# Two-layer graph attention: gathered rows in a ring of 24, and VectorE's masks ahead in layer 0's first steps

## Chip, cores and metric

One core of a Trainium2 chip. The metric is the device time of one launch in microseconds. The core's engines are TensorE (PE; PEld is its weight load), VectorE (DVE), ScalarE (ACT), GpSimd (POOL) and SyncE (SP, which only issues transfers). Each works through its own list of instructions in order, and semaphores order them against each other.

## What is computed

Two attention layers over a graph of 8192 nodes with 256 features. The adjacency (8192 x 8192, int32) is symmetric and sparse: about 8 neighbours a row, and the node itself.

```python
h = jnp.maximum(_layernorm(x), 0.0)
Wh = h @ W
e = (Wh @ a[:256])[:, None] + (Wh @ a[256:])[None, :]
att = softmax(where(adj == 0, -1e9, e), axis=1)
x = x + leaky_relu(att @ Wh, 0.2)                    # layer 0
h = jnp.maximum(_layernorm(x), 0.0)
e = leaky_relu(h @ a1[:256] + (h @ a1[256:]).T, 0.01)
att = softmax(where(adj > 0, e, -9e15), axis=1)
x = x + att @ h                                      # layer 1
```

## The kernel before

Nodes go in 64 tiles of 128 rows. All order on an engine is written out by hand, in the order in which the Python code emits the instructions.

**Layer 0** takes tile t per step. SyncE loads the tile's adjacency in four quarters of 1 MB; ScalarE converts them (`convert`) to eight-bit floats; VectorE folds eight adjacency columns into one byte in four parts (`fold`, parts 0 to 3); TensorE transposes the folded words (`turn`, four transposes), ScalarE copies them out (`copy_words`), and VectorE unpacks them into the masks `adjT` with eight operations (`unpack`). TensorE multiplies these masks with the 64 tiles of V in 128 matmuls (`aggregate`, L973); the turn of the next tile, t + 1, stands inside, behind matmul pair `turn_at`, and waits for the last fold part of tile t + 1 (L963). An aggregate of tile t waits for `adjT_ready` of t and for `ysb_ready` of t - 2, which is ScalarE's copy of the sums off the accumulator that t will reuse (L975 to L977; `copy_sums` L528).

VectorE's `step(t)` (L838) does, in order: `normalise(t-1)`, a reciprocal behind the sums of tile t - 1; fold part 0 of t + 2, behind its conversion; `extract(t+1)`, the neighbour lists out of the keys; `add_x(t-1)`, behind `copy_sums`; `unpack(t+1)`, behind `copy_words`; parts 1 and 2; `scale_h`, behind ScalarE's root; part 3; `decode`, one list of a group of four, and for every fourth tile also the bits of all four (steps 2, 6, 10 and so on); `make_keys(t+2)`; `dots(t-1)`, behind ScalarE's `finish`. ScalarE's step (L535) has the quarters of t + 3 with `copy_words(t+1)`, `copy_sums(t-1)`, the root and `finish` between them: quarter 0, words, sums, quarter 1, root, quarter 2, finish, quarter 3.

**Between the layers** the 44 tiles from tile 20 on are sorted by number of neighbours.

**Layer 1** does the first 20 tiles as dense attention on TensorE and the other 44 by gathering each node's neighbours. The dense part runs over 5 groups of 4 tiles, each in 16 chunks of 64 matmuls, 80 chunks in all. For each chunk ScalarE makes signs (L1300), in two halves, each waiting for TensorE to be done with the half four back; VectorE makes the negative and the positive mask (L1473, L1478); TensorE waits for the positive mask (L1620) and multiplies (L1639).

The gathered part has 420 rows of slots (a slot is one neighbour of each of 128 nodes): 24 in the first tile of nodes, down to 4 in the last. GpSimd issues one indirect DMA per slot (L1264), 128 x 258 numbers, into `gat`. They are grouped in 88 batches of at most 6 (`BS`); batch k lies in buffer k mod 4 (`NBUF`), and before its first gather GpSimd waits until the batch four back has been added (L1262). ScalarE takes the two exponentials of a batch (`weights`, L1313), VectorE their larger (`larger`, L1509) and then, per slot, adds the weighted row (`add_row`, L1518); `rows_by` says how many rows VectorE has added by each chunk, some 5 a chunk (7 in the first 16), put around the negative and the positive mask. `LEAD = 3` is by how many rows the weights go ahead. The sum of a finished tile is closed in the next tile's rows 2 to 4 (`join`, `divide`, `add_x1`, which raises `so_ready`). GpSimd scatters a finished tile to the output (`scatter`, L1253, waits for `so_ready`) after it has issued the batch that stands `OUT_LAG = 5` batches behind the tile's last (L1268).

## Time and profile before

| | before |
|---|---|
| median of 3 runs | 1916.56 us (1912.78 to 1921.1) |
| profiled execution | 1914.35 us, of it 1912.5 us span |
| TensorE busy | 1691.5 us (88%), granted clock 0.93 of full |
| VectorE busy | 1203.0 us (63%) |
| ScalarE busy | 973.4 us (51%) |
| GpSimd busy | 651.6 us (34%) |

Layer 0's projection and statistics fill the first 105 us, its 64 tiles stand from 105 to 1058, layer 1 from 1067 to the end. The page cuts the span in 40 slices of 48 us:

```profile
PE   6888999999999999999999397677888888978878
DVE  7488888988888888674444377652435445435434
ACT  5987665665666556666662375432333233323322
POOL 0000000000000000026665548755656657665562
PEclk9998999999999999999999698877889889979889
```

A digit is the busy share of the slice in tenths. PE is full in most of layer 0 and isn't in layer 1, where the clock row shows that it also ran below full clock. A busy share alone doesn't say what bounds a stage: that is read from which wait ends last.

### The profile page before, as it was taken

How to read it: one execution, taken by the hardware profiler on the slowest of the kernel's cores; microseconds unless marked ns; L12 is line 12 of the kernel's file. 1: busy time of each engine (PE TensorE's matmuls, PEld its weight loads, DVE VectorE, ACT ScalarE, POOL GpSimd, SP SyncE). 2: the span in 40 equal slices, each digit the busy share in tenths (PEclk: the TensorE clock that was granted, in tenths of full speed). 3: DMA queues.
4: the chain of work that ended last, by engine and by line, in shares of the span. 5: the costliest groups of instructions: out<-in, count | busy, mean ns of one | idle time of the engine just before them, and what ended most of it. 6: DMA issues, size and time to landing. Idle time of an engine off the chain costs nothing. (4 is left out here: it accounts for less than half of the span.)

```text
span 1912.5 us, 37724 instructions
## 1 busy us (share of the span) xinstructions
PE 1691.5 (88%) x13955; PEld 1391.3 (73%) x13955; DVE 1203.0 (63%) x4595; ACT 973.4 (51%) x1367; POOL 651.6 (34%) x607
## 2 busy tenths in 40 slices
PE   6888999999999999999999397677888888978878
PEld 5646888888888888888888285454666667757657
DVE  7488888988888888674444377652435445435434
ACT  5987665665666556666662375432333233323322
POOL 0000000000000000026665548755656657665562
PEclk9998999999999999999999698877889889979889
DMA  8529998888988889989994534533333333433331
GB/s 287 182 76 386 342 349 325 314 311 321 354 320 326 318 310 331 355 333 378 386 379 104 130 94 134 160 80 88 101 89 83 111 89 94 117 100 99 88 92 52
DMA packets 142801, 410.60 MB, mean 215 GB/s; under 512 B 26193, under 2 KB 90066, under 8 KB 109906
## 3 DMA queue, kind: packets, MB, share of 16 engines
q1 hardware_dynamic: 108434, 329.85, 47.6%
q0 software_dynamic: 27904, 73.43, 13.9%
q10 hardware_dynamic: 6336, 5.77, 1.0%
q8 instruction: 62, 1.02, 0.2%
q14 instruction: 65, 0.53, 0.1%
HBM read 368.94 MB, written 40.03 MB: 214 GB/s over the span
## 5 line engine op out<-in xcount | busy, mean ns | idle before, releaser
L984 PE MATMUL banks<-HV,adjT 128*128 128x257 f16 x8192 | 938.8, 274 | 16.7 <-DVE adjT L658 8.8
L984 PEld LDWEIGHTS banks<-HV,adjT 128*128 128x128 fp8e4 x8192 | 792.5, 98 | 148.2 <-DVE HV L688 23.7
L1639 PE MATMUL banks<-Vp,adjp 128*128 128x257 f16 x2560 | 540.6, 292 | 115.4 <-issue 59.2
L1639 PE MATMUL banks<-Vn,adjn 128*128 128x257 f16 x2560 | 538.1, 291 | 48.9 <-issue 47.7
L1264 POOL DMA_INDIRECT gat<-h_of_layer,rec x420 | 465.8, 1109 | 275.5 <-issue 117.9
L444 ACT ACTIVATE adj_f<-adj_i 128x2048 fp8e4<-128x2048 int32 x256 | 480.1, 1898 | 6.6 <-DMA adj_i<-in_adj 6.5
L1300 ACT ACTIVATE adjn<-h1bc,nh 128x512 fp8e5<-128x512 f32 x320 | 212.1, 716 | 446.2 <-remote 272.1
L1639 PEld LDWEIGHTS banks<-Vp,adjp 128*128 128x128 fp8e4 x2560 | 261.2, 103 | 192.3 <-issue 126.5
L1639 PEld LDWEIGHTS banks<-Vn,adjn 128*128 128x128 fp8e4 x2560 | 262.2, 103 | 124.8 <-issue 76.5
L425 POOL DMA_DIRECT2D HV<-x_after_layer x44 | 25.5, 580 | 773.4 <-DVE rank L911 741.3
L1473 DVE TENSOR_TENSOR adjn<-adjp,adjn 128x1024 uint16<-128x1024 uint16 x80 | 55.4, 692 | 334.8 <-ACT adjn L1300 296.0
L1534 DVE SCALAR_TENSOR_TENSOR sacc<-gat,w,sacc 128x257 f32<-128x257 f32 x332 | 152.5, 477 | 0.0
L492 ACT ACTIVATE pk<-banks 128x512 uint16<-128x512 uint16 x64 | 37.9, 593 | 170.3 <-PE banks L969 143.9
L695 DVE RECIPROCAL rden<-banks 128x1 f32<-128x1 f32 x64 | 10.7, 168 | 145.9 <-PE banks L984 115.3
L655 DVE TENSOR_SCALAR adjT<-pk 128x512 uint16<-128x512 uint16 x448 | 94.6, 282 | 0.0
L957 PE MATMUL banks<-w_sb,hT 128*128 128x257 f32 x256 | 68.9, 392 | 15.6 <-ACT hT L456 15.3
L627 DVE SCALAR_TENSOR_TENSOR fold<-adj_f 128x1024 int32<-128x1024 int32 x64 | 77.2, 1206 | 7.4 <-ACT adj_f L444 7.4
L418 POOL DMA_INDIRECT x_after_layer_sorted<-HV,rank x44 | 66.5, 1512 | 13.4 <-issue 12.2
L525 ACT ACTIVATE hh<-x,nmr,rstd 128x256 f32<-128x256 f32 x64 | 38.4, 601 | 53.6 <-DVE nmr L727 45.8
L1515 DVE TENSOR_TENSOR w<-e 128x5 f32<-128x5 f32 (+2 forms) x88 | 13.9, 157 | 77.8 <-ACT e L1321 58.5
L519 ACT ACTIVATE std<-mv,eps 128x1 f32<-128x1 f32 x64 | 18.8, 294 | 86.0 <-DVE mv L719 83.9
L1255 POOL DMA_INDIRECT out<-sout,rec x44 | 46.5, 1058 | 43.1 <-DVE sout L1550 31.8
(158 smaller groups left out, 1395.2 us busy)
## 6 DMA issues: line engine op xcount, KB each, us to landing
adj_i<-in_adj SPq DMA_DIRECT2D x256, 1024.0 KB
h_of_layer<-hh SPq DMA_DIRECT2D x64, 129.0 KB
hs<-h_of_layer SPq DMA_DIRECT2D x64, 129.0 KB
xt<-in_x SPq DMA_DIRECT2D x64, 128.0 KB
packed_adj<-pk SPq DMA_DIRECT2D x64, 128.0 KB
x_after_layer<-x SPq DMA_DIRECT2D x64, 128.0 KB
HV<-in_x SPq DMA_DIRECT2D x14, 512.0 KB, 8.8
gat<-h_of_layer,rec POOLq DMA_INDIRECT x420
```

Source lines behind the costliest of these rows:

```text
L418: pool.indirect_dma_start(x1s_d, bass.IndirectOffsetOnAxis(ap=rank[:, m:m + 1], axis=0), HV[:, T + m % SH, 0:D], None).then_inc(xs_out[m % ...
L444: nc.scalar.activation(adj_f[:, b, q * QC:(q + 1) * QC], adj_i[:, q, :], ACT.Copy, scale=2.0, saturate=False).then_inc(conv_done, 1)
L627: nc.vector.scalar_tensor_tensor(four, whole[:, 0:4 * GW], 1, whole[:, 4 * GW:8 * GW], ALU.logical_shift_right, ALU.bitwise_or)\
L655: last = nc.vector.tensor_scalar(adjT[:, b, i, :], pk[:, pb, :], PAIR << i, 6 - i, ALU.bitwise_and, ALU.logical_shift_left)
L957: last = nc.tensor.matmul(wps[t % 3][:, 0:DV], hT[:, t % 2, c, :], w_sb[:, c, :], start=(c == 0), stop=(c == 1))
L984: last = nc.tensor.matmul(acc[b][:, 0:DV], adjT_h[:, b, i, q, :, h], V0[:, jb, s, 0:DV], start=(jb == 0 and s == 0), stop=(jb == T - 1 and ...
L1255: pool.indirect_dma_start(out, bass.IndirectOffsetOnAxis(ap=rec[:, m, OWN:OWN + 1], axis=0), sout[:, m % NOUT, :], None).then_inc(so_out[m ...
L1264: pool.indirect_dma_start(gat[:, k % NBUF, s - s0, :], None, h_d, bass.IndirectOffsetOnAxis(ap=rec[:, m, s:s + 1], axis=0))\
L1300: i = nc.scalar.activation(adjn_b[:, c % 2, jb // 2, :, jb % 2], h1bc[:, g2, :], ACT.Relu, scale=-BIG, bias=nh2[:, tiles[j]:tiles[j] + 1], ...
L1473: nc.vector.tensor_tensor(part, both, part, ALU.bitwise_and).then_inc(neg_ready, 1)
L1534: nc.vector.scalar_tensor_tensor(acc, x, w, acc, ALU.mult, ALU.add)\
L1639: mm = nc.tensor.matmul(bank[2 * i + part][:, 0:DV], m[:, i * P:(i + 1) * P], V[:, j, s, 0:DV], start=(j == 0 and s == 0), stop=(j == T - ...
```

## The change

Two parts, one in each layer.

In layer 0, VectorE's steps 1 to 6 (`HURRY = 7`) put `unpack(t+1)`, `extract(t+1)` and fold part 0 of t + 2, in that order, behind `normalise`, ahead of `add_x`. And TensorE's turns inside tiles 2 and 3 stand behind matmul pair 48 and 32 of 64, not behind pair 4; tile 1's stays at 48, and from tile 4 on it is pair 4 again.

In layer 1, `gat` becomes a ring of 24 rows. The gather of row q waits until row q - 24 has been added, one wait per row. A batch that would cross the ring's end is cut there, which makes 101 batches of the 88. `NBUF = 6` batches have a landing semaphore each, and a batch also waits until the one six back has been added. `lead_of` lets the weights of a batch go ahead only when the batch before it has begun. Three semaphores of `take_sums` become one.

```diff
--- before.py
+++ after.py
@@ -82,6 +82,7 @@
     XB = 4
     LAG = 5
     XL = 1
+    HURRY = 7
     UN = 4
     VU = 16
     NPK = 4
@@ -836,15 +837,19 @@
                         decode_end(e)
 
                 def step(t, j, n_in, x1_reuse, kept, off, ahead=True, folds=True, listed=False,
-                         taken=False, e=None):
+                         taken=False, e=None, hurry=False):
 
                     normalise(t - 1, (j - 1) % 2)
-                    if folds:
+                    if hurry:
+                        unpack(t + 1, (j + 1) % 2, (j + 1) % NPK)
+                        extract(t + 1, (j + 1) % UN)
                         fold(t + 2, j % 2, 0)
-                    if taken:
+                    elif folds:
+                        fold(t + 2, j % 2, 0)
+                    if taken and not hurry:
                         extract(t + 1, (j + 1) % UN)
                     add_x(t - 1, (j - 1) % NX, n_in, x1_reuse, kept, off)
-                    if ahead:
+                    if ahead and not hurry:
                         unpack(t + 1, (j + 1) % 2, (j + 1) % NPK)
                     if folds:
                         fold(t + 2, j % 2, 1)
@@ -922,7 +927,7 @@
                 dve.wait_ge(hh_ones, 1)
                 for t in range(1, T):
                     step(t, t % UN, *counts(t), ahead=t + 1 < T, folds=t + 2 < T, listed=t + 2 < NS,
-                         taken=t + 1 < NS, e=(t - 2) // UN if 2 <= t < NS + 2 else None)
+                         taken=t + 1 < NS, e=(t - 2) // UN if 2 <= t < NS + 2 else None, hurry=t < HURRY)
                     if t == SORT:
                         sort_totals()
                     if t == SORT + 1:
@@ -1001,7 +1006,9 @@
                 pe.wait_ge(ones_set, 2)
                 aggregate(0, 0, v0_wait=True, reuse=False, turn_at=None)
                 aggregate(1, 1, reuse=False, turn_at=3 * T // 4)
-                with pe.Fori(1, SORT // 2) as k:
+                aggregate(2, 0, turn_at=3 * T // 4)
+                aggregate(3, 1, turn_at=T // 2)
+                with pe.Fori(2, SORT // 2) as k:
                     for b in range(2):
                         aggregate(k * 2 + b, b)
                 for b in range(2):
@@ -1032,7 +1039,8 @@
         RB = 4
         BIG = 2.0 ** 100
         BS = 6
-        NBUF = 4
+        RING = 24
+        NBUF = 6
         LEAD = 3
         FIRST = 1.35
         HEAD = 3.0
@@ -1044,7 +1052,10 @@
         for m in range(NS):
             parts = -(-slots[m] // BS)
             for i in range(parts):
-                batch.append((m, slots[m] * i // parts, slots[m] * (i + 1) // parts))
+                s0, s1 = slots[m] * i // parts, slots[m] * (i + 1) // parts
+                q = sum(slots[:m])
+                wrap = -(-(q + s0 + 1) // RING) * RING - q
+                batch.extend([(m, s0, s1)] if wrap >= s1 else [(m, s0, wrap), (m, wrap, s1)])
         row = [(m, s, k) for k, (m, s0, s1) in enumerate(batch) for s in range(s0, s1)]
         begin = [row.index((m, s0, k)) for k, (m, s0, s1) in enumerate(batch)]
         at = [sum(slots[:m]) for m in range(NS + 1)]
@@ -1056,7 +1067,8 @@
 
         def lead_of(q):
 
-            return sum(1 for b in begin if b < q + LEAD) if q < len(row) else len(batch)
+            return sum(1 for k, b in enumerate(begin)
+                       if b < q + LEAD and (k == 0 or begin[k - 1] < q)) if q < len(row) else len(batch)
 
         def ended(q):
 
@@ -1097,7 +1109,7 @@
             sS = early[:, 9 * T:9 * T + 2 * NS].rearrange("p (s t) -> p s t", s=2)
             tS = early[:, 11 * T:11 * T + NS]
             exc = early[:, 12 * T:12 * T + NS]
-            gat = sb("gat", [P, NBUF, BS, ROW], f32)
+            gat = sb("gat", [P, RING, ROW], f32)
             sacc = sb("sacc", [P, 2, 2, DV], f32)
             sout = sb("sout", [P, NOUT, D], f32)
             e8 = sb("e8", [P, 2, 2, BS], f32)
...
@@ -1258,11 +1268,13 @@
 
                 done = 0
                 for k, (m, s0, s1) in enumerate(batch):
-                    if k >= NBUF:
-                        pool.wait_ge(row_added, begin[k - NBUF + 1])
                     for s in range(s0, s1):
+                        q = at[m] + s
+                        free = max(q - RING + 1, begin[k - NBUF + 1] if k >= NBUF and s == s0 else 0)
+                        if free > 0:
+                            pool.wait_ge(row_added, free)
                         pool.indirect_dma_start(
-                            gat[:, k % NBUF, s - s0, :], None, h_d,
+                            gat[:, q % RING, :], None, h_d,
                             bass.IndirectOffsetOnAxis(ap=rec[:, m, s:s + 1], axis=0))\
                             .then_inc(gat_in[k % NBUF], 16)
                     while done < NS and last[done] + OUT_LAG <= k:
@@ -1318,7 +1330,7 @@
                     if k >= 2:
                         act.wait_ge(w8_ready, k - 1)
                     for i, scale in ((0, 1.0), (1, SLOPE1)):
-                        nc.scalar.activation(e8[:, k % 2, i, 0:s1 - s0], gat[:, k % NBUF, 0:s1 - s0, DV],
+                        nc.scalar.activation(e8[:, k % 2, i, 0:s1 - s0], gat[:, begin[k] % RING:begin[k] % RING + s1 - s0, DV],
                                              ACT.Exp, scale=scale, bias=hb[:, i, m:m + 1]).then_inc(e8_ready, 1)
 
                 def load_rows(m):
...
@@ -1523,7 +1535,7 @@
                     acc = sacc[:, m % 2, s % 2, :]
                     if i == 0:
                         dve.wait_ge(w8_ready, k + 1)
-                    x = gat[:, k % NBUF, i, 0:DV]
+                    x = gat[:, q % RING, 0:DV]
                     w = w8[:, k % 2, i:i + 1]
                     if s < 2:
                         if m >= 2 and s == 0:
```

## Rows read from the trace of the kernel before

**Rows 1.** windows of stages: length, busy us (instructions) per engine, clock, DMA share, GB/s

```profile
155.80:172.40 16.60, 16.59 (x131) 13.81 (x132) 14.46 (x59) 13.38 (x12) 0.00 (x0) 0.86 1.02 415
...
200.00:1058.00 858.00, 858.00 (x7798) 749.63 (x7797) 645.65 (x2860) 513.59 (x460) 137.74 (x132) 1.00 0.88 323
1330.00:1870.00 540.00, 458.54 (x3517) 355.53 (x3516) 238.76 (x701) 173.86 (x356) 336.46 (x316) 0.88 0.35 97
```

**Rows 2.** timeline, TensorE: start us, length us, what, count, idle before and releaser

```profile
145.97 1.05 PE L984 MATMUL banks<-HV,adjT 128*128 128x257 f16 x8
155.81 1.45 PE L984 MATMUL banks<-HV,adjT 128*128 128x257 f16 x6 [8.78 <-DVE adjT L658]
...
188.18 0.38 PE L969 MATMUL banks<-idb,fold 128*128 128x128 bf16 x4
```

**Rows 3.** timeline, VectorE, layer 0's steps 1 to 3

```profile
148.77 1.22 DVE L627 SCALAR_TENSOR_TENSOR fold<-adj_f 128x1024 int32<-128x1024 int32 x1 [6.67 <-ACT adj_f L444]
149.92 0.42 DVE L749 MAX8 ktop<-HV 128x8 f32<-128x256 f32 x1
...
152.42 0.42 DVE L706 SCALAR_TENSOR_TENSOR lr<-ysb 128x256 f32<-128x256 f32 x1
...
153.89 1.47 DVE L655 TENSOR_SCALAR adjT<-pk 128x512 uint16<-128x512 uint16 x7
...
159.18 0.17 DVE L695 RECIPROCAL rden<-banks 128x1 f32<-128x1 f32 x1
...
168.54 0.16 DVE L781 TENSOR_REDUCE fl<-ktop 128x1 f32<-128x8 f32 x1
...
177.54 0.67 DVE L647 TENSOR_TENSOR HV<-fold,keypos 128x512 f32<-128x512 uint16 x1
...
179.06 0.17 DVE L695 RECIPROCAL rden<-banks 128x1 f32<-128x1 f32 x1
```

**Rows 4.** timeline, ScalarE, the same steps

```profile
143.71 0.60 ACT L492 ACTIVATE pk<-banks 128x512 uint16<-128x512 uint16 x1 [0.29 <-PE banks L969]
...
151.35 0.46 ACT L532 ACTIVATE ysb<-banks,rden 128x256 f32<-128x256 f32 x1
...
162.04 0.58 ACT L492 ACTIVATE pk<-banks 128x512 uint16<-128x512 uint16 x1
```

**Rows 5.** timeline, VectorE, the first row added in layer 1

```profile
1110.61 0.35 DVE L1531 TENSOR_SCALAR sacc<-gat,w 128x257 f32<-128x257 f32 x1
```

**Rows 6.** timeline, GpSimd, two stretches of layer 1

```profile
1121.54 1.15 POOL L1264 DMA_INDIRECT gat<-h_of_layer,rec  x1 [22.88 <-DVE sacc L1534]
...
1124.39 3.28 POOL L1264 DMA_INDIRECT gat<-h_of_layer,rec  x1 [0.30 <-issue]
...
1403.01 0.94 POOL L1264 DMA_INDIRECT gat<-h_of_layer,rec  x1 [6.42 <-DVE sacc L1534]
...
1411.36 0.97 POOL L1264 DMA_INDIRECT gat<-h_of_layer,rec  x1 [0.30 <-issue]
```

**Rows 7.** who waited for whom, 1050 to 1913: us in total, times, longest

```profile
PEld banks L1639 <- issue: 203.0, 212, 15.6
...
POOL gat L1264 <- DVE sacc L1534: 115.8, 25, 22.9
...
POOL out L1255 <- DVE sout L1550: 31.8, 7, 10.8
```

**Rows 8.** windows between two stops of GpSimd, columns as above

```profile
1406.00:1409.00 3.00, 3.00 (x30) 2.62 (x28) 3.00 (x9) 0.22 (x2) 2.39 (x3) 1.00 0.50 150
...
1415.00:1418.00 3.00, 1.40 (x10) 0.79 (x9) 0.00 (x0) 0.00 (x0) 2.26 (x3) 1.00 0.32 89
```

**Rows 9.** the page's costliest groups: busy, mean ns of one, idle before

```profile
L1264 POOL DMA_INDIRECT gat<-h_of_layer,rec x420 | 465.8, 1109 | 275.5 <-issue 117.9
...
L1515 DVE TENSOR_TENSOR w<-e 128x5 f32<-128x5 f32 (+2 forms) x88 | 13.9, 157 | 77.8 <-ACT e L1321 58.5
```

**Rows 10.** instructions that touch the tile gat: ns min/median/max

```profile
L1321 ACT ACTIVATE e<-gat,hb x176: 282/287/310, 1082.7 to 1884.1; 128x5 f32<-128x5 f32 x66, 128x4 f32<-128x4 f32 x60, 128x6 f32<-128x6 f32 x40, 128x3 f32<-128x3 f32 x10
```

More of the change, by code:

```diff
@@ L1153, in two_layer_graph_attention @@
             evn_ready = sem("evn_ready")
-            den2_ready = sem("den2_ready")
-            den_ready = sem("den_ready")
-            rd_ready = sem("rd_ready")
+            den_steps = sem("den_steps")
             fac_ready = sem("fac_ready")
@@ L1483, in take_sums @@
                                             banks[:, :, D].rearrange("p (g s) -> p s g", s=2), ALU.mult)\
-                        .then_inc(den2_ready, 1)
-                    dve.wait_ge(den2_ready, g + 1)
+                        .then_inc(den_steps, 1)
+                    dve.wait_ge(den_steps, g * 3 + 1)
                     nc.vector.tensor_tensor(den[:, :], den2[:, 0, :], den2[:, 1, :], ALU.add)\
-                        .then_inc(den_ready, 1)
-                    dve.wait_ge(den_ready, g + 1)
-                    nc.vector.reciprocal(rd[:, :], den[:, :]).then_inc(rd_ready, 1)
-                    dve.wait_ge(rd_ready, g + 1)
+                        .then_inc(den_steps, 1)
+                    dve.wait_ge(den_steps, g * 3 + 2)
+                    nc.vector.reciprocal(rd[:, :], den[:, :]).then_inc(den_steps, 1)
+                    dve.wait_ge(den_steps, g * 3 + 3)
                     for s in range(2):
```

## Prediction, made blind

> **What bounds the kernel now.** I read the windows by stage first. From 200 to 1058 us TensorE never stops: 7798 matmuls in 858 us, 0.110 us each, at full clock [rows 1]. That is nearly all of layer 0, so a change there pays only through its start, before 200 us, and whatever TensorE loses there is never won back. The one hole is in front of tile 2: TensorE ends tile 1 at 147.0 and starts tile 2 at 155.8, released by the last of the eight mask operations [rows 2]. The tile then takes 16.6 us at a mean clock of 0.86 [rows 1] instead of the usual 132 x 0.110 = 14.5 (128 matmuls and the turn's four), so the hole cost 8.8 + 2.1 = 10.9 us. That is all the layer 0 part can win.
>
> Layer 1 is different. From 1330 to 1870 TensorE makes 3517 matmuls, 55 of the 80 chunks of 64, in 540 us: 9.8 us a chunk where 64 x 0.110 = 7.0 would do [rows 1]. The list of waits says what is missing: weight loads stood 203.0 us on "issue", with nothing to wait for, and GpSimd stood 115.8 us in 25 stops for rows to be added [rows 7]. The two belong together. In 1406 to 1409, shortly after a stop, GpSimd gathers and TensorE makes 10 matmuls a us; in 1415 to 1418, with GpSimd gathering at its quickest and VectorE idle, it makes 3.3 [rows 8]. By the timelines, each long slow stretch ends 1 to 3 us after GpSimd stops at its buffer limit. So there is a cycle: GpSimd runs, TensorE starves, no rows are added, the buffer fills, GpSimd stops, TensorE recovers. A gather is on GpSimd for 1.11 us in the mean [rows 9] and 0.30 us lie between two [rows 6]; 420 gathers and 44 scatters ask some 464 x 1.41 = 654 us of layer 1's 845 (1067 to 1912). GpSimd is nearly a second bound.
>
> **Layer 0, step 1.** Today VectorE's order is fold part 0 (which waits for converted adjacency until 148.8), extraction 149.9 to 152.4, add_x to 153.9, masks to 155.5 [rows 3]. The mask words lie ready at 144.3 [rows 4]. With masks first, they are done by 144.3 + 1.6 = 145.9, before tile 1 ends. What is late next: tile 2 also waits for the copy of tile 0's sums off its accumulator, and that ScalarE instruction runs 151.35 to 151.8, behind conversions that the change doesn't move [rows 4]. Tile 2 starts at 151.8, not 155.8: 4.0 us won, not 8.8. With a hole of 4.8 us I leave the cold-clock loss at 2.0 (bounds 0 and 2.1).
>
> **Steps 2 and 3, by the durations of [rows 3].** The turn of tile 3 now sits at 3/4 of tile 2, so at 151.8 + 10.9 + 2.0 = 164.7, its word copy (0.6 us) at 165.3; today the copy is done at 162.6 [rows 4]. VectorE finishes step 1 at 159.2 as today (its dots wait for ScalarE), and in the new order the next thing in its queue is masks 3, waiting for that copy. Queued behind them are extraction, fold 4, add_x and the decoding, and VectorE idles 6 us that it uses today. Then: masks to 166.9, extraction 2.5, fold part 0 1.15, add_x 1.7, parts 1 and 2 0.9, scale and part 3 0.8, making 173.9; decoding, 168.5 to 177.5 today, 9.0, and keys and dots 1.5: step 2 ends at 184.4, today 179.1. Tile 3 runs 168.0 to 182.6; masks 4 come at 184.4 + 1.7 = 186.1 (today they are 1 us ahead of tile 4). TensorE waits 3.5 us. Tile 4's turn comes 1.1 us into the tile, 187.2, and needs the finished fold 5. Its part 3 comes after extraction, part 0, add_x, parts 1 and 2 and scale: 186.1 + 7.0 = 193.1. Today it is ready half a us ahead of the turn at 188.2 [rows 2]. TensorE waits 5.9 us more. Tile 5 starts at about 206.2 with the clock's ramp, today 201.6: 4.6 us late. The next decoding of bits, in step 6, is still in the new order and costs tile 8 about 2 us again by the same sum. Layer 0 ends 6 to 8 us later than today. I take +7. If the turn of tile 5 did not wait, it would be about -1; if ScalarE's queue moved forward too, -8.
>
> **Layer 1, first release.** GpSimd stops after 24 gathers, at 1098.7, and goes on at 1121.5, when a batch of six is added [rows 6]. The first row is added at 1110.6 + 0.35 = 1111.0 [rows 5]; by the new rule gather 24 needs that row alone. Then each row frees one gather. VectorE waits for rows in 1138 to 1226, where GpSimd never stops, so the head start is kept: -10 us (bounds 0 and -10.5).
>
> **Layer 1, the ring in steady work.** The limits follow from the lists of rows in the code. Before, a batch's first gather needs the batch four earlier added: GpSimd is held 16.1 rows ahead on average for rows 200 to 299, 13.0 for 300 to 379. The ring alone would give 21.5 and 17.7. But the scatter of a finished tile stands five batches after its last batch on GpSimd's queue, and batches are cut at the ring's end: 101, not 88. Five batches are then fewer rows. The scatter of tile 22, say, stands after 290 gathers instead of 294, and needs the same row 277 added (it waits for the finished tile, five rows into the next). Behind it every gather waits. With this limit the means are 19.2 and 15.3, and at 40 of the 44 scatters the scatter is the tighter limit (21 before). So GpSimd is still stopped once a tile, which is about two chunks: as often as today, where 26 stops of over 1 us fall on these 55 chunks. No row is late there today, so that being further ahead feeds nobody. Value taken: 0. Bounds: each of some 25 stops could end on the first add of a chunk instead of the fifth, 4 x 0.4 = 1.6 us earlier, -40; or each of some 20 slow stretches could last one gather more, 1.25 us, of which TensorE loses 1.1: +22.
>
> **Small parts.** 13 more batches: two exponentials of 0.29 us [rows 10] and a maximum of 0.16 [rows 9] each, 9.6 us in all on ScalarE and VectorE, which both wait for TensorE in most chunks; taken +3, bounds 0 and 10. 300 more waits on GpSimd: the gather at 1411.4, a batch's first, has a satisfied wait before it and follows after the same 0.30 us as the others [rows 6], so nothing. One semaphore for three: same waits, nothing.
>
> Sum: 1914.35 + 7 - 10 + 0 + 3 = 1914.4 for the profiled execution. The median of the runs stands 2.2 above it, and I allow one more us for the second start of the clock after tile 4: 1917.5.
>
> **The Trainium skill.** A gather takes 0.94 us when VectorE idles and up to 3.28 when it is busy [rows 6]. The Trainium skill, "DMA: Bandwidth & Descriptors", section on SWDGE vs HWDGE vs iDMA, says that GpSimd writes the descriptors into SBUF state from which VectorE locks it out in its two-port mode; by that rule the trace agrees. On the slow stretches it speaks against my reading: "Runtime: NRT & Kernel Launch", section Instruction fetch mechanics, calls the crossing of a block of instructions mostly hidden. By that rule gathers would not starve TensorE, the depth of the ring would be worth nothing either way, and the sum would be the same as mine; the 203.0 us on "issue" [rows 7] say that something isn't hidden.
>
> **Rivals.** (B) Finer stops end the starving. A stop of 1 to 2 us is enough today to give TensorE 10 us of full pace; if the ring keeps GpSimd at its limit, every chunk has a short stop and the long slow stretches go. For it: the pace right after stops. Against it: the scatters. Half of the bound, -20: 1894 to 1898. (C) Slower, by one mechanism: in 1330 to 1870 the deeper ring lets GpSimd run on when TensorE is already starved, one gather more in each of 20 stretches, +22: 1917.5 + 22 = 1939; it decides from about half a gather more, when with layer 0's +7 the kernel is past +0.5%. For it: stretches end only with the stop, and were longest, about 25 us around 1240 and 1300, where GpSimd had most room. Against it: the scatter stops it once a tile. (D) Layer 0 does what the diff says: tile 2 at 151.8 and no later hole, -5 with a warm clock: 1905. Against it: the 6 us that VectorE idles. That the change doesn't do what it says is half of my forecast: the ring of 24 is held at 9 to 19 by the scatters.
>
> **Chances.** Forecast 0.46 (1908 to 1927), B 0.24, C 0.23, D 0.07. What a measurement here can tell from no change is about 0.5%, 9.6 us. Faster by more: B's 0.21, D's 0.05, 0.03 of the forecast: 0.29. Slower by more: C's 0.20 and 0.06 of the forecast: 0.26. Within: 0.45. The range leaves out the ends of B and C: 1893 to 1937.
>
> **What would show it.** Tile 2 starting at 151.8 after the copy of sums; a wait of 3 to 4 us before tile 4 and of 5 to 6 at its turn; layer 0 ending 6 to 8 us later. Gather 24 at about 1111 from layer 1's same start. In steady work, waits of GpSimd's scatter for the finished tile, 31.8 us in 7 today [rows 7], up to over 60 in more than 15, and "issue" of the weight loads within 20 us of 203. The prediction is wrong if "issue" falls by half (B) or rises by 20 (C), or if layer 0 shows no new hole.

## The result, and the profile after

The change makes the kernel slower: 1965.64 us, median of 5 runs (1952.13 to 1967.12), against 1917.0 for the kernel before beside it (5 runs), a ratio of 1.0225 with a 95% interval of 1.0178 to 1.0271. The whole interval is above 1, so it is slower; whether by less or more than 2% is open. The forecast was 1917.5 with a range that ended at 1937. The profiled execution took 1959.8 us, 45.5 more than before's 1914.35.

The page after, its line of TensorE, of GpSimd and of the granted clock in 40 slices of 49 us:

```profile
PE   6887999999999999999997588678788688877678
POOL 0000000000000000046672587855556455455552
...
PEclk9998999999999999999999789879899798878779
```

Layer 0 looks as before. In layer 1 TensorE shows more 6s and 7s, and in the last nine slices the clock shows three 7s where the kernel before has one. The windows of the same trace split it. Columns: stretch in us, its length, busy time and instructions of each engine, clock, DMA share, GB/s. Layer 1 is cut some 3 us before chunk 40 of 80 begins, at 1507 here and at 1518 in the kernel before:

```profile
1074.00:1507.00 433.00, 331.70 (x2527) 256.38 (x2528) 229.77 (x651) 183.41 (x402) 278.81 (x245) 0.86 0.42 113
1507.00:1949.00 442.00, 342.04 (x2593) 260.86 (x2591) 175.46 (x521) 126.51 (x268) 231.51 (x220) 0.84 0.29 82
1330.00:1870.00 540.00, 424.65 (x3278) 328.01 (x3277) 223.41 (x657) 165.46 (x351) 300.90 (x284) 0.87 0.32 88
```

The kernel before, cut at the same chunk (its row for 1330 to 1870 is in [rows 1]):

```profile
1067.00:1518.00 451.00, 341.85 (x2535) 260.16 (x2536) 228.42 (x645) 181.16 (x392) 285.15 (x252) 0.83 0.41 111
1518.00:1909.00 391.00, 331.10 (x2587) 260.06 (x2584) 177.82 (x527) 124.30 (x257) 227.43 (x213) 0.89 0.33 90
```

The first half got quicker, 451 to 433 us for the same 2530 matmuls. The second went from some 385 us (1518 to the last matmul at 1903.6) to 442 for the same 2590. Layer 1 as a whole, from its first gather to its last matmul, takes 874.7 us instead of 836.1, and it starts 7.0 us later (1074.5 instead of 1067.5). That is 45.6 us, all of the loss: 7 from layer 0, 18 won in the first half of layer 1, 57 lost in the second. The sum is firm. The split between the halves isn't: e1 below has the layer 1 of the kernel before and splits it otherwise.

The waits say who stands in it (engine, line, releaser: us in total, times, longest). The lines answer to [rows 7]:

```profile
PEld banks L1651 <- issue: 231.4, 254, 10.0
POOL out L1265 <- DVE sout L1562: 195.0, 30, 13.7
POOL gat L1276 <- DVE sacc L1543: 25.5, 8, 11.7
POOL gat L1276 <- DVE sacc L1546: 22.3, 47, 6.3
```

GpSimd's waits before a scatter rose from 31.8 us in 7 to 195.0 in 30, and its waits at a gather fell from 115.8 in 25 and 41.8 in 10 to 22.3 and 25.5. So the scatter is the limit now, once a finished tile. The weight loads' "issue" rose from 203.0 to 231.4.

**What a long run of GpSimd does to TensorE.** GpSimd's timeline around one scatter interval (start, length, operation, and in brackets the idle time before it and what ended it):

```profile
1714.24 1.19 POOL L1265 DMA_INDIRECT out<-sout,rec  x1 [4.34 <-DVE sout L1562]
...
1749.81 0.95 POOL L1276 DMA_INDIRECT gat<-h_of_layer,rec  x1 [0.30 <-issue]
1764.31 1.86 POOL L1265 DMA_INDIRECT out<-sout,rec  x1 [13.56 <-DVE sout L1562]
```

From 1714 to 1751 it never stops, and then it waits 13.6 us for a finished tile. The same stretch by windows of 4 us:

```profile
1722.00:1726.00 4.00, 4.00 (x39) 3.49 (x37) 1.35 (x4) 2.29 (x6) 2.93 (x4) 1.00 0.48 132
1726.00:1730.00 4.00, 4.00 (x37) 3.33 (x35) 1.77 (x5) 1.14 (x4) 3.09 (x4) 1.00 0.39 102
1730.00:1734.00 4.00, 1.65 (x9) 0.88 (x9) 3.00 (x11) 1.34 (x2) 3.39 (x3) 0.89 0.39 108
1734.00:1738.00 4.00, 3.36 (x15) 1.86 (x13) 0.00 (x0) 0.00 (x0) 3.09 (x4) 0.50 0.49 148
1738.00:1742.00 4.00, 2.73 (x12) 1.36 (x11) 0.00 (x0) 0.00 (x0) 3.01 (x4) 0.50 0.40 108
1742.00:1746.00 4.00, 1.36 (x6) 0.57 (x5) 0.73 (x3) 1.72 (x4) 2.86 (x4) 0.50 0.46 128
1746.00:1750.00 4.00, 0.58 (x2) 0.10 (x1) 2.10 (x6) 0.00 (x0) 3.09 (x4) 0.50 0.39 103
1750.00:1754.00 4.00, 1.15 (x5) 0.49 (x5) 0.00 (x0) 0.07 (x1) 0.76 (x1) 0.50 0.30 66
1754.00:1758.00 4.00, 4.00 (x25) 2.97 (x23) 0.00 (x0) 1.26 (x2) 0.00 (x0) 0.63 0.00 0
1758.00:1762.00 4.00, 4.00 (x39) 3.49 (x37) 1.64 (x5) 2.48 (x8) 0.00 (x0) 1.00 0.00 0
```

TensorE makes 39 matmuls in 4 us, then 9, 15, 12, 6, 2 and 5, and comes back to 39 only when GpSimd's column is 0. Nothing holds it that the profile can name. VectorE and ScalarE have little to do, the DMA engines are less than half busy, and the clock has dropped to its lower level (0.50) after TensorE began to idle, which makes the way back longer (25 in its first 4 us). This is the cycle of the prediction's first part, but with 27 gathers and scatters in one run.

How the long ones weigh: I counted the starts of the matmuls in steps of 2 us and summed the stretches in which TensorE made fewer than 5 a us, each at its length less 0.110 us a matmul. In the second half they cost the kernel before 86 us, of them 16 in the one stretch that lasted 15 us or more. In the changed kernel they cost 137, of them 109 in six such stretches, up to 28 us long. Of the 57 us that the second half lost, 51 are in such stretches.

The length of a run isn't all that counts. From 1183 to 1291 GpSimd goes 108 us without a stop of over 0.6 us, and TensorE falls and comes back several times in it, with GpSimd at work all the while:

```profile
1236.00:1240.00 4.00, 4.00 (x39) 3.49 (x37) 0.80 (x2) 2.81 (x8) 3.39 (x3) 1.00 0.94 274
1240.00:1244.00 4.00, 0.56 (x6) 0.25 (x3) 0.73 (x3) 0.49 (x2) 3.04 (x4) 1.00 0.77 251
```

In 1252 to 1256 it is at 37 again. It often comes back behind long gathers beside a busy VectorE (two of 2.6 us in the mean in 1232 to 1236). From 1268 on, with VectorE idle from 1272, it stays under 10 matmuls in 4 us until GpSimd stops. What lets it come back is open.

### The profile page after: what moved, and what is told of

Same layout as the page of the kernel before. It is cut to its first block and busy times, and to the rows that moved or that the text cites. A ratio compares the mean times of both kernels' runs of the same rounds, so it can differ in the third digit from the quotient of the medians.

```text
span 1957.8 us, 37793 instructions
## 1 busy us (share of the span) xinstructions
PE 1696.0 (87%) x13955; PEld 1389.5 (71%) x13955; DVE 1207.3 (62%) x4608; ACT 978.4 (50%) x1393; POOL 641.8 (33%) x607
## 5 line engine op out<-in xcount | busy, mean ns | idle before, releaser
L1276 POOL DMA_INDIRECT gat<-h_of_layer,rec x420 | 457.8, 1090 | 159.2 <-issue 111.4
L1265 POOL DMA_INDIRECT out<-sout,rec x44 | 52.2, 1186 | 200.3 <-DVE sout L1562 195.0
L1527 DVE TENSOR_TENSOR w<-e 128x5 f32<-128x5 f32 (+5 forms) x101 | 16.0, 159 | 95.8 <-ACT e L1333 75.9
L1333 ACT ACTIVATE e<-gat,hb 128x5 f32<-128x5 f32 (+5 forms) x202 | 46.5, 287 | 38.4 <-DMA gat<-h_of_layer,rec 38.4
```

Source lines behind the costliest of these rows:

```text
L1265: pool.indirect_dma_start(out, bass.IndirectOffsetOnAxis(ap=rec[:, m, OWN:OWN + 1], axis=0), sout[:, m % NOUT, :], None).then_inc(so_out[m ...
L1276: pool.indirect_dma_start(gat[:, q % RING, :], None, h_d, bass.IndirectOffsetOnAxis(ap=rec[:, m, s:s + 1], axis=0))\
L1333: nc.scalar.activation(e8[:, k % 2, i, 0:s1 - s0], gat[:, begin[k] % RING:begin[k] % RING + s1 - s0, DV], ACT.Exp, scale=scale, bias=hb[:, ...
```

## The experiments

Two kinds of chip turned up, told apart by what the kernel before takes. On one (the runs above, e1 to e4, e17 and e18) it takes 1916 to 1926 us. On the other (e5 to e16, three chips) it takes 1752. Every ratio is against the kernel before on the same chip.

For each kernel I also give the time that TensorE lost in the steady part of layer 1, from 1130 us to its last matmuls: the window's length less 0.110 us a matmul, the full pace of [rows 1]. For the kernel before and the changed one that is 773 - 4827 x 0.110 = 242 and 819 - 4885 x 0.110 = 282 us:

```profile
1130.00:1903.00 773.00, 634.25 (x4827) 489.60 (x4825) 368.32 (x1059) 267.90 (x565) 480.61 (x436) 0.87 0.36 100
```

```profile
1130.00:1949.00 819.00, 641.27 (x4885) 492.09 (x4883) 376.87 (x1088) 278.98 (x603) 479.43 (x435) 0.86 0.34 94
```

**One part alone: e1_layer0 and e2_ring.** e1 is the kernel before with layer 0's part of the diff. e2 is the changed kernel with that part undone:

```diff
-                         taken=t + 1 < NS, e=..., hurry=t < HURRY)
+                         taken=t + 1 < NS, e=..., hurry=False)
-                aggregate(2, 0, turn_at=3 * T // 4)
-                aggregate(3, 1, turn_at=T // 2)
-                with pe.Fori(2, SORT // 2) as k:
+                with pe.Fori(1, SORT // 2) as k:
```

> The kernel before with the layer 0 part alone. My step by step sum, which the trace after bears out (tile 2 starts early, then waits before tile 4 and in it), says layer 0 ends 6 to 8 us later and layer 1 is as before: 1922 to 1926 us where before has 1917. Rival: the start of layer 1 changes the course of its starving and recovering, and the time moves by more than 15 us.

> The kernel after with layer 0 put back as it was: the ring alone. If the parts add up, 1965.6 - 7 = 1955 to 1962 us. In the profile, GpSimd's scatter waits for the finished tile some 30 times and 190 us in all, and between such waits TensorE has slow stretches of over 15 us.

e1: 1929.68 us against 1915.67, ratio 1.0071 (1.0032 to 1.0110). e2: 1940.54 us, ratio 1.0119 (1.0049 to 1.0190). Both parts cost time, and their sum, 1.9%, agrees with the whole change's 2.25% within the intervals. e1's profiled execution is 12.6 us over before's (1926.93 and 1914.35): layer 1 starts 9.0 us later (1076.5 for 1067.5) and takes 3.6 us more (839.7 for 836.1, TensorE lost 248 us instead of 242). The median is 14 us over, where 5 to 9 were asked; the interval, 6 to 21 us, holds the 9 of layer 0's own stage, so a further price in layer 1 isn't shown. The ring's part is cheaper than expected (1955 to 1962 was asked of e2), but it has the changed kernel's marks:

```profile
PEld banks L1649 <- issue: 222.0, 249, 15.6
POOL out L1263 <- DVE sout L1560: 163.1, 24, 16.2
```

TensorE lost 264 us in it, between 242 and 282.

e1 also says how far one trace of layer 1 can be trusted. Its layer 1 is that of the kernel before, and yet chunk 40 begins 436 us after the first gather and the rest takes 404; in the kernel before it is 454 and 382, in the changed kernel 436 and 439. So the 18 us that the changed kernel won in its first half come without the ring too, and the halves move by some 20 us between executions of the same code. Layer 1 as a whole is steadier: 836.1 and 839.7 us without the ring, 874.7 and 857.8 (e2) with it. The same count of slow stretches over the whole steady part, for the runs on this kind of chip (each is a range, by where the steps of 2 us begin), beside the unbroken runs of GpSimd that lasted over 30 us, from 1330 us on (a stop of up to 1 us doesn't break a run):

| | slow stretches, us | of them in stretches of 15 us and over | GpSimd runs over 30 us |
|---|---|---|---|
| before | 201 to 208 | 57 to 87 | 1 |
| e1_layer0 | 209 to 213 | 49 to 70 | 1 |
| after | 237 to 248 | 131 to 145 | 4 |
| e2_ring | 223 to 226 | 91 to 119 | 5 |
| e3_scatter | 186 to 197 | 55 to 83 | 1 |
| e4_ahead14 | 181 to 188 | 27 to 63 | 2 |

e3 and e4 are the next two runs.

**The place of the scatters, and the depth: e3_scatter and e4_ahead14.** e3 is e2 with each scatter directly behind a wait that the ring makes anyway, so that no scatter brings a wait of its own in the steady part. e4 is e3 with GpSimd held 14 rows ahead instead of 24:

```diff
+        AHEAD = 24          # e4: 14
-                        free = max(q - RING + 1, begin[...] if ... else 0)
+                        free = max(free, q - AHEAD + 1, begin[...] if ... else 0)
                         if free > 0:
                             pool.wait_ge(row_added, free)
+                        while done < NS - 1 and free >= at[done + 1] + min(4, slots[done + 1] - 1) + 1:
+                            scatter(done)
+                            done += 1
...
-                    while done < NS and last[done] + OUT_LAG <= k:
-                        scatter(done)
-                        done += 1
```

> e2_ring with one edit: a scatter stands right behind the ring's own wait for the same row, so that it never holds GpSimd back further than the ring does. Ring, cuts and 101 batches stay. Theory S (the scatters turn the limit of 23 rows into a saw-tooth from 9 to 23, and GpSimd's long unstopped runs up the tooth starve TensorE): the long stretches go, 1885 to 1920 us. Theory D (being further ahead is itself the harm): GpSimd is now always about 23 ahead, so as slow as e2_ring or slower, 1955 to 1980. Theory B (the 13 extra batches cost it): as e2_ring, 1955 to 1962.

> e3_scatter with one number changed: GpSimd may be 14 rows ahead instead of 24, by the same wait per row. Theory S: what counts is that it stops often, not how far ahead: the same as e3_scatter within 15 us, 1885 to 1920. Theory D: faster than e3_scatter by 40 us or more, since it is less far ahead than ever before. If 14 rows are too few, VectorE's waits for weights go from 60 us to over 120 us and the time is over 1930.

e3: 1910.35 us, ratio 0.9968 (0.9935 to 1.0000). e4: 1891.13 us, ratio 0.9856 (0.9804 to 0.9907), faster than both kernels. Moving the scatters alone gives back 30 us of e2's time. The same 24 rows are there and the same 101 batches, so neither the ring's size nor the cut batches are the cause. The scatter theory asked for 1885 to 1920, the two others for 1955 and more. The waits of e3 and, below it, of e4:

```profile
PEld banks L1650 <- issue: 182.8, 229, 8.4
POOL gat L1278 <- DVE sacc L1545: 78.0, 45, 7.7
POOL out L1264 <- DVE sacc L1545: 44.3, 15, 8.2
```

```profile
PEld banks L1650 <- issue: 189.3, 238, 15.8
POOL gat L1278 <- DVE sacc L1545: 71.6, 57, 7.6
POOL gat L1278 <- DVE sacc L1542: 61.7, 19, 12.7
```

Now the gathers wait in many short stops (e4: 76 at a gather, 133 us), TensorE lost 229 us in each, and issue fell below before's 203. A limit of 14 is worth another 19 us by the medians, more than the scatter theory asked (15 at most) and half of what depth as the cause would have given (40). The steady part of the two traces doesn't show it, since e3's profiled execution was the quickest of its ten (1897.23).

Where the limit of 14 does show is the start of layer 1. Nothing has been added there, and GpSimd issues 24 gathers in a row (before) or 14 (e4). The same 4 us of the kernel before and of e4, whose first gathers went at 1067.5 and 1069.9:

```profile
1092.00:1096.00 4.00, 0.75 (x2) 0.21 (x2) 0.00 (x0) 0.00 (x0) 3.08 (x4) 0.53 0.75 117
1092.00:1096.00 4.00, 4.00 (x39) 3.49 (x37) 2.46 (x9) 2.91 (x7) 0.00 (x0) 1.00 0.40 112
```

Chunk 2 begins 44.7 us after the first gather in the kernel before (39 to 44 in e1, e2, e3 and the changed kernel, which all issue 24) and 30.7 us in e4. Of the 26 us by which e4's layer 1 is shorter than before's (810.2 and 836.1), 14 stand there, and 11 of them are left at chunk 10.

**Where TensorE doesn't starve: e5_uncut14, e8_masks1, e9_after, e10_ahead14, e16_ahead10.** e5 is the kernel before, 88 batches and four buffers, with e4's limit of 14 and its place of the scatters. e8 puts the masks first in step 1 alone (`HURRY = 2`, all turns as before). e9 is the changed kernel again and e10 is e4 again. e16 is e4 with `AHEAD = 10`.

> The kernel before with two edits in layer 1's GpSimd list: a wait per row that lets GpSimd be 14 rows ahead at most (its batch wait stays), and scatters behind that wait. Four buffers and 88 uncut batches as before. If the extra cuts cost nothing, the same as e4_ahead14, 1885 to 1898; if 13 batches cost their 9.6 us, 1875 to 1885; if it is the ring itself that helps e4_ahead14, 1905 or more.

> The kernel before with the masks first in step 1 alone, and TensorE's turns where they were. Step 1 by itself wins 4 us at tile 2; the turn of tile 3, one us into tile 2, then waits for the fold until about 157, and VectorE, which is late by then, sets tile 5 as before. Layer 0 ends within 2 us of before: 1913 to 1919. If the whole loss of e1_layer0 came from step 1, it would be 1925 or more.

> The changed kernel once more, beside the same kernel before as the next three. One chip gives the kernel before 1916 us and the other on which runs were made gives it 1752, with next to no stretches in which TensorE starves while GpSimd gathers (issue of the weight loads 43.6 us in e5). If this chip starves TensorE (before near 1916): ratio 1.022 to 1.029, issue 225 to 240 us, GpSimd's waits for the finished tile over 150 us. If it doesn't (before near 1752): theory S, by which layer 1's loss is TensorE starved in the long runs that the scatters allow, expects that only layer 0's part is left, 1.002 to 1.010, issue under 50; theory T, by which the scatters delay the rows themselves and the chip's kind doesn't matter, expects 1.020 to 1.030 here too.

> e4 once more, the ring held at 14 rows ahead and each scatter behind the ring's own wait for the same row, layer 0 as before. If this chip starves TensorE: 0.980 to 0.991 of the kernel before, issue 180 to 195. If it doesn't: theory S (all that the limit does is to take long starved stretches away) expects 0.998 to 1.006, since there is nothing to take away and the first release saves what 13 batches more cost; theory T expects 0.980 to 0.991 here too.

> e4 with the limit at 10 rows ahead instead of 14. 24 gave 1910 us and 14 gave 1891. If this chip starves TensorE and every row of room less takes from the starved stretches, 1870 to 1885 (ratio 0.977 to 0.984) and issue under 185; if rows come late before that helps, 1890 to 1930 with VectorE's waits for the exponentials over 150 us. If it doesn't starve: slower than before by 1 to 3%, since there the rows are what is late.

| | us | before beside it | ratio | 95% interval |
|---|---|---|---|---|
| e5_uncut14 | 1761.74 | 1751.88 | 1.0056 | 1.0036 to 1.0076 |
| e8_masks1 | 1755.42 | 1751.88 | 1.0011 | 0.9995 to 1.0027 |
| e9_after | 1755.44 | 1752.25 | 1.0014 | 0.9991 to 1.0037 |
| e10_ahead14 | 1762.01 | 1752.25 | 1.0051 | 1.0029 to 1.0073 |
| e16_ahead10 | 1839.78 | 1752.52 | 1.0492 | 1.0467 to 1.0516 |

The changed kernel costs 0.14% there, which the interval doesn't tell from nothing, and not 2.25%. That is a little under what the starving theory asked (1.002 to 1.010) and far from the other's 1.020. e4's gain of 1.4% is a loss of 0.5%, as that theory allowed. So the loss and the gain are both of TensorE starving. Here is the changed kernel on that kind of chip, 40 us in which GpSimd gathers without a stop, and its waits:

```profile
1400.00:1420.00 20.00, 20.00 (x183) 17.46 (x181) 10.75 (x32) 9.07 (x18) 15.43 (x16) 1.00 0.56 168
1420.00:1440.00 20.00, 20.00 (x183) 17.46 (x181) 12.82 (x37) 8.36 (x19) 15.73 (x15) 1.00 0.37 104
```

```profile
DVE w L1527 <- ACT e L1333: 173.5, 69, 7.2
PEld banks L1651 <- issue: 41.5, 19, 8.0
POOL out L1265 <- DVE sout L1562: 7.6, 5, 4.5
```

183 matmuls in 20 us are the full pace, beside 15 or 16 gathers. TensorE lost 89 us in the steady part (610 - 4734 x 0.110), GpSimd waits 7.6 us for finished tiles, and VectorE waits for rows instead. I take GpSimd to be the bound there, so that a limit of 14 or 10 only delays it: e10 lost 100 us and e16 172 (4.9% slower, where 1 to 3% was expected). The start of layer 1 fits too: 24 gathers in a row cost nothing here, chunk 2 begins 31.6 us after the first in e9 and 30.3 in e10. There is no run of e16 on the other kind of chip, so whether 10 would beat 14 there is open. e8's trace agrees with its tie: tile 2 starts at 154.3, and its turn then stands 2.57 us for the last fold. So masks first pay nothing that can be measured in step 1 alone either.

e15_uncut14 is e5 once more, on the same kind of chip again:

> The kernel before with its 88 batches and four buffers, a wait per row that holds GpSimd at most 14 rows ahead, and each scatter behind that wait. If this chip starves TensorE: if e4's gain comes from the limit and the place of the scatters, 0.980 to 0.992 of before; if it comes from the ring with its cut batches and its first release, 0.995 to 1.005. If it doesn't: 1.003 to 1.008, as e5.

1763.45 us, ratio 1.0065 (1.0043 to 1.0087), as e5. Whether the limit brings its gain without the ring is therefore open.

**Are the gathers the cause, and which side of them? e17_no_gathers and e18_narrow.** Both are e4 with the gathers changed. e17 issues only the first 24, and e18 fetches 43 numbers instead of 258 behind the first 24, from other rows of h than the layer's. In both the first 24 all fetch the first neighbour. The main lines:

```diff
e17:
-                        pool.indirect_dma_start(
+                        if q < RING:
+                            pool.indirect_dma_start(
e18:
+                        part = slice(0, ROW) if q < RING else slice(0, 43)
-                            gat[:, q % RING, :], None, h_d,
+                            gat[:, q % RING, part], None, h_d if q < RING else h_d.rearrange("r (k c) -> (r k) c", c=43),
```

> e13 again: e4 without the gathers behind the first 24, so the output isn't the layer's. If this chip starves TensorE (before near 1916): theory G (the gathers starve it) expects issue under 20 us and 1690 to 1760 us; theory P (a reason of TensorE's own) expects issue over 120 us and a time over 1830. If it doesn't (before near 1752): 0.967 to 0.973 of before.

> e14 again: e4 with 43 instead of 258 numbers in each gathered row behind the first 24, so the output isn't the layer's. If this chip starves TensorE: theory D (the gathers' number starves it) expects issue within 25 us of 189 and a time within 20 us of 1891; theory W (their bytes starve it) expects issue under 80 us and a time under 1811. If it doesn't: 1.000 to 1.006 of before.

Both ran on a chip that starves (before 1925.6 us). e17: 1696.95 us, ratio 0.882 (0.8719 to 0.8921). Its issue is 26.8 us, a little over the 20 asked for, and TensorE lost 39 us. e18: 1906.66 us, ratio 0.9902 (0.9859 to 0.9945), with issue at 170.4. The same 310 us of both and of e4, in the order e17, e18, e4:

```profile
1330.00:1640.00 310.00, 303.74 (x2735) 264.12 (x2733) 188.86 (x565) 140.46 (x298) 27.56 (x25) 1.00 0.12 38
```

```profile
1330.00:1640.00 310.00, 255.70 (x1996) 199.38 (x1995) 139.10 (x404) 99.61 (x206) 187.94 (x178) 0.90 0.16 38
```

```profile
1330.00:1640.00 310.00, 263.39 (x2042) 202.27 (x2042) 140.01 (x407) 102.12 (x210) 193.82 (x181) 0.90 0.35 97
```

Without gathers TensorE makes 2735 matmuls and its clock stays at 1.00. With narrow ones it makes 1996, hardly other than 2042 with whole rows, although the DMA engines' share has gone from 0.35 to 0.16 and the traffic from 97 to 38 GB/s. In the steady part it lost 248 us (e4 229). So the gathers starve TensorE, and by their being issued, not by their bytes. Whether it is their number, GpSimd's work on each or something that goes with both, these runs don't separate.

The same two edits had run before on the other kind of chip, without gathers as e6, e11 and e13, narrow as e7, e12 and e14:

> e4_ahead14 without the gathers after the first 24 rows (and these 24 all fetch the first neighbour), so its output is not the layer's: VectorE and ScalarE weigh and add what lies in the ring. If GpSimd's gathers are what starves TensorE, the weight loads' idle time on issue falls from 190 us to under 40, chunks take 7.1 to 7.6 us, and the time is 1660 to 1710 us. If the cause lies in TensorE's own instruction stream or in VectorE's and ScalarE's order, the slow stretches stay and the time is over 1780.

> e4_ahead14 with gathers of 43 numbers a row instead of 258 after the first 24 (from h seen as rows of 43, so wrong rows, and the output is not the layer's): one sixth of the bytes, as many instructions and descriptors. Theory issue (the descriptors that GpSimd writes are what starves TensorE): as e4_ahead14, 1880 to 1900, with issue still at 150 to 200 us. Theory bytes (the moved data are): 1700 to 1780, with issue under 80.

> e10 without the gathers behind the first 24, so the rows added are old ones and the output isn't the layer's. If this chip starves TensorE: theory G (the gathers starve it) expects issue under 20 us and 1690 to 1760 us, 130 to 200 less than e10; theory P (TensorE is slow in these stretches for a reason of its own: its clock, its own fetching, the dense part's waits) expects issue still over 120 and at most 60 us less. If it doesn't: 0.965 to 0.975, as e6.

> e10 with 43 instead of 258 numbers in each gathered row behind the first 24, so the output isn't the layer's: as many gathers and descriptors with a sixth of the bytes. If this chip starves TensorE: theory D (the number of descriptors, or GpSimd's writing of them, starves it) expects issue within 25 us of e10's and the time within 20 us; theory W (the bytes, which fill the DMA engines, starve it) expects issue under 80 us and at least 80 us less than e10. If it doesn't: within 0.5% of e10, as e7's profiled execution was within 0.5% of e5.

> e4 without the gathers behind the first 24, so the output isn't the layer's. If this chip starves TensorE (before near 1916): theory G (the gathers starve it) expects issue under 20 us and 1690 to 1760 us; theory P (a reason of TensorE's own) expects issue over 120 us and a time over 1830. If it doesn't (before near 1752): 0.967 to 0.973 of before, as e6 and e11.

> e4 with 43 instead of 258 numbers in each gathered row behind the first 24, so the output isn't the layer's: as many gathers and descriptors with a sixth of the bytes. If this chip starves TensorE: theory D (their number starves it) expects issue within 25 us of 189 and a time within 20 us of 1891; theory W (their bytes starve it) expects issue under 80 us and a time under 1811. If it doesn't: 0.998 to 1.006 of before, as e7 and e12.

Without gathers: 1699.74, 1699.51 and 1701.07 us, ratios 0.9695, 0.9697 and 0.9698. Narrow: e12 1759.58 (1.0031, 1.0005 to 1.0057) and e14 1759.34 (1.0033, 1.0018 to 1.0049), with issue at 40.9 and 48.5 us as in e10 with whole rows (41.5). Of e7's two executions one took 1756.96 us and the other 6685.42, which nothing here explains, and its median isn't used. Without gathers the two kinds of chip are alike, 1697 and 1700 us. So the 165 us between them arise only beside the gathers.

## Why the prediction was wrong, step by step

**Layer 0: the term was right, +7, its split wasn't.** TensorE's timeline of the changed kernel, where tile 0 starts 0.7 us earlier than before. It answers to [rows 2]:

```profile
150.49 13.81 PE L989 MATMUL banks<-HV,adjT 128*128 128x257 f16 x98 [4.19 <-issue]
186.24 1.76 PE L989 MATMUL banks<-HV,adjT 128*128 128x257 f16 x10 [3.83 <-DVE adjT L659]
193.01 0.59 PE L974 MATMUL banks<-idb,fold 128*128 128x128 bf16 x4 [5.02 <-DVE fold L642]
193.40 16.26 PE L989 MATMUL banks<-HV,adjT 128*128 128x257 f16 x128
```

Tile 2 at 150.5 (predicted 151.8), 3.83 us in front of tile 4 (3.5), the turn of tile 5 at 193.0 after 5.0 us (193.1 after 5.9): the queue behind the masks worked as worked out. Tile 5 came at 208.4, not 206.2, since the 128 matmuls behind the turn took 16.3 us instead of 14.1, a second start of the clock. The prediction left it out of the 206.2, which is 193.1 and 118 full-pace matmuls, and put it at one us in the last sum. The further 2 us at tile 8 never came: its masks end at 251.6 and it starts at 252.0. So two errors of 2 us cancel, and that the term came out at 7 is in part luck. From tile 0 on, tile 20 is 7.7 us later than before. Rival D is out. Layer 1 starts 7.0 us later in the changed kernel and 9.0 in e1.

**First release: right as an event, its worth not shown.** It answers to [rows 6]:

```profile
1117.34 0.94 POOL L1276 DMA_INDIRECT gat<-h_of_layer,rec  x1 [11.70 <-DVE sacc L1543]
1121.31 0.94 POOL L1276 DMA_INDIRECT gat<-h_of_layer,rec  x1 [3.02 <-DVE sacc L1543]
```

Gather 24 goes 42.9 us after gather 0, before 54.1 us: 11.2 earlier, 10 predicted. Whether TensorE won them isn't shown. Chunk 16 begins 185.4 us after the first gather in the changed kernel and 203.6 in the kernel before, but 189.0 in e1, which has no ring. On the kind of chip that doesn't starve, the changed kernel's layer 1 (e9) is 5.5 us shorter than that of the kernel before (in e8): 670.5 and 676.0.

**Small parts: right as far as they can be seen.** ScalarE is busy 978.4 us (973.4 before) and VectorE 1207.3 (1203.0), 9.3 us more together where 9.6 were worked out. No per-row wait shows a price: a gather still follows in 0.30 us. Nor do the 13 batches, where TensorE doesn't starve: e5 and e15 without them are at 1.0056 and 1.0065, e10 with them at 1.0051.

**The ring in steady work: the step that failed.** The term was 0, with -40 and +22 as its ends. In the profiled execution layer 1 takes 38.6 us more, and if the first release is worth its 11, that leaves +50 for the steady work, small parts included: 7 - 11 + 50 is the 46 measured. If it is worth nothing, the term is +39, still above its upper end; in e2, with the ring alone, layer 1 takes 21.7 us more (18.1 more than e1's). The prediction had the cause in its hands. It worked out that at 40 of 44 scatters the scatter is the tighter limit, and that GpSimd stops at it once a tile, and both came true. It then took the mean number of rows ahead (16.1 to 19.2, 13.0 to 15.3) and the number of stops (some 25) and concluded that little changes. But neither is what costs. A limit that is put once per tile is a saw-tooth. By the lists of rows in the code, for tiles 20 to 35, GpSimd may be 9 to 16 rows ahead right behind a tile's scatter and 16 to 24 before the next; in the kernel before it gains at most 5 rows between two waits. So it waits long, and then runs long. In the run of 36 us TensorE's pace fell from 39 matmuls to 2 per 4 us, and 24 gathers in a row at the start of layer 1 cost 14 us where 14 cost none, so I take it that one run of 36 us costs more than two of 18. The number of stops of over 1 us in the second half is nearly the same (18, before 21); their spread isn't: four runs of GpSimd of over 30 us after 1330 where the kernel before has one, and six slow stretches of 15 us and more in the second half where one stood. That the scatters do it is shown by e3, which moves nothing else and is 30 us faster than e2.

**Rival C had the right mechanism at less than half its price.** It gave each of 20 stretches one gather more, 22 us. What came was not every stretch a little longer but a few much longer: in the second half 93 us more in those of 15 us and over, 42 less in the shorter ones, 51 net. Its counter-argument, "the scatter stops it once a tile", was the cause itself. C gave 1939, with layer 0's +7 already in it, and 1965.6 was measured. "Issue" rose by 28.4 us, over the 20 that the prediction named as C's mark.

**Rival B** asked for short stops in every chunk. With the scatters moved, e3 and e4 come near it (59 and 76 stops at a gather), and e4 is 1.4% faster: its mechanism is real where TensorE starves, though half of e4's gain stands at the start of layer 1, and the scatters in their old place keep it out of this change.

**The page's rule.** On the kind of chip that starves, e4 took 1891 us with its gathers and 1697 without (e17). The Trainium skill, "Runtime: NRT & Kernel Launch", section Instruction fetch mechanics, calls the crossing of a block of instructions mostly hidden. If TensorE's instructions came as smoothly as that beside gathers too, gathers would cost it nothing in this way, and the measurement there shows a cost. That it is the fetching isn't shown either. I only know that no resource which the profile lists is full in these stretches.

## What to carry to other kernels

A mean distance between producer and consumer doesn't price a limit, where long unbroken runs do the harm: look at the longest run that each limit allows, and put every wait of the same queue, the scatters' too, behind the limit that is meant to rule. An engine with slack that hurts another by running should be stopped often and briefly; whether it hurts at all can differ from chip to chip, so measure such a change on more than one. And compare such a stage as a whole: parts of it moved by 20 us here between executions of the same code.

## What the runs showed of the hardware

- The same kernel takes 1916 us on one kind of chip and 1752 on the other, at the same time in layer 0 (layer 1's first gather at 1067.5 to 1069.9 in both, where layer 0 is as before). Without gathers both take 1697 to 1701.
- On the first kind, in the stretch from 1714 to 1764 of the changed kernel, TensorE's pace fell from 39 matmuls per 4 us to 2. It began to fall some 16 us after GpSimd's last stop, beside gathers one behind the other (0.95 us each at their quickest, 0.30 apart), and it was back at 39 in the second 4 us after 1754, GpSimd's last gather having ended at 1750.8. In a run of 108 us it fell and came back several times. On the second kind it stays at 183 matmuls in 20 us beside such gathers.
- A sixth of the bytes per gathered row changes little in that (issue 170.4 us against 189.3, 248 us lost against 229).
- What in TensorE's path the gathers hold, and how the two kinds of chip differ, is open. A pause between gathers wasn't tried.
